# Within each slot of the attention, the value products and exponentials are placed ahead of the output projection

## The reference, cut to what matters

```
x = x + attention(layernorm(x))                # x: 8 sequences of 512 tokens, width 256
    q, k, v = x @ W.T + b                      # 16 query heads, 4 key/value heads, 16 wide
    q, k = rope(q), rope(k)
    att = softmax(causal(q @ k.T / 4))
    y = att @ v
    return y @ Wo.T + bo
x = x + ffn(layernorm(x))
    top 8 of 64 experts per token, softmax of their logits as weights
    out = sum of weight * down(silu(gate(x)) * up(x)) + a shared expert
```

## Time and profile before

| | us |
|---|---|
| median of 3 runs | 1220.87 (1215.87 to 1222.19) |
| the profiled execution | 1212.77 |
| its span, first to last instruction | 1211.0 |
| PE busy | 1023.7 (85%) |
| DVE busy | 710.7 (59%) |
| ACT busy | 676.3 (56%) |
| POOL busy | 723.8 (60%) |

### The profile page before, as it was taken

The page is one execution under the profiler, slowest core; times in us unless marked ns, Lnnn a source line. Parts: engine busy times, 40 slices in busy tenths (PEclk is TensorE's granted clock), DMA queues, the critical chain, the costliest instruction groups (busy, mean ns, idle before and its releaser), DMA issues. The chain is left out here.

```text
span 1211.0 us, 24260 instructions
## 1 busy us (share of the span) xinstructions
PE 1023.7 (85%) x7378; PEld 809.7 (67%) x7378; DVE 710.7 (59%) x2229; ACT 676.3 (56%) x1650; POOL 723.8 (60%) x954
## 2 busy tenths in 40 slices
PE   2799989899989898898998611999999999999962
PEld 1466666666666666666665401999989889999950
DVE  2466776767767677777674550222236656666666
ACT  2366665666656656666554101777656667766630
POOL 3111122774856847658367775577777777777770
PEclk9689999999999999999898855999999999999985
DMA  2388876821312313212132994777778989998735
GB/s 89 131 261 278 270 250 209 285 100 44 112 56 80 118 32 110 83 58 97 39 133 81 323 321 155 217 220 219 219 265 313 374 307 339 316 357 282 260 111 187
DMA packets 142157, 233.23 MB, mean 193 GB/s; under 512 B 17271, under 2 KB 119878, under 8 KB 136656
## 3 DMA queue, kind: packets, MB, share of 16 engines
q1 hardware_dynamic: 67216, 101.06, 25.8%
q0 software_dynamic: 27648, 69.28, 15.8%
q10 hardware_dynamic: 47168, 61.35, 15.3%
HBM read 107.32 MB, written 132.66 MB: 198 GB/s over the span
## 5 line engine op out<-in xcount | busy, mean ns | idle before, releaser
L1363 POOL DMA_INDIRECT res_d<-y,dst_i x320 | 321.6, 1005 | 111.0 <-issue 82.8
L453 POOL DMA_INDIRECT rows_d<-pay,slot_i x256 | 258.4, 1009 | 73.4 <-issue 67.8
L858 DVE TENSOR_REDUCE nmax<-ps 128x1 f32<-128x512 f32 (+3 forms) x448 | 225.6, 530 | 103.7 <-PE ps L508 101.8
L724 ACT ACTIVATE wgu_s<-ps 128x512 f32<-128x512 f32 x320 | 191.3, 599 | 108.2 <-PE ps L508 105.0
L508 PE MATMUL ps<-mask,ident_b 128*128 128x256 bf16 (+1 forms) x640 | 172.2, 269 | 0.0
L501 PE MATMUL ps<-kT,qT 96*128 96x512 f32 (+3 forms) x512 | 166.8, 388 | 6.2 <-DVE nmax L858 4.0
L1294 PE MATMUL psB<-wgu_s,xT 128*128 x1280 | 171.9, 278 | 0.0
L1311 PE MATMUL psD<-wdp_s,innerT 128*128 x640 | 165.7, 382 | 3.7 <-ACT innerT L1199 2.5
L548 PE MATMUL ps<-qT,kT 128*128 128x512 f32 (+3 forms) x512 | 161.3, 377 | 0.9 <-ACT qT L737 0.6
L1294 PEld LDWEIGHTS psB<-wgu_s,xT 128*128 128x128 f32 x1280 | 158.2, 195 | 0.4 <-issue 0.4
L1118 DVE TENSOR_TENSOR inner<-inner,psB 128x128 f32<-128x128 f32 x160 | 45.7, 286 | 188.9 <-ACT inner L1193 185.6
(11 more groups left out here) (241 smaller groups left out, 1622.3 us busy)
## 6 DMA issues: line engine op xcount, KB each, us to landing
rows_d<-blank ACTq DMA_DIRECT2D x8, 5440.0 KB, 19.4
xg<-rows_d SPq DMA_DIRECT2D x160, 272.0 KB
yk<-res_d SPq DMA_DIRECT2D x32, 1024.0 KB
wgu_s<-wgu_in ACTq DMA_DIRECT2D x8, 1024.0 KB, 13.5
xs<-x_d SPq DMA_DIRECT2D x32, 192.5 KB
x_d<-x SPq DMA_DIRECT2D x30, 192.5 KB, 2.5
res_d<-y,dst_i POOLq DMA_INDIRECT x320
wgu_s<-x_in SPq DMA_DIRECT2D x32, 128.0 KB, 2.1
```

The costliest lines, as they stand in the source:

```text
L453: pool.indirect_dma_start(rows_d, bass.IndirectOffsetOnAxis(ap=slot_i[par][:, t, k:k + 1], axis=0), pay[par][:, t, :], None).then_inc(s_sc ...
L724: act.activation(pexp[p % 4][:, s, :], ps2[:, (5 * p + s) % 2, :], ACT.Exp, scale=HEAD_D ** -0.5).then_inc(s_exp, 1)
L858: return dve.tensor_reduce(nmax[u][:, tile, heads[0]:heads[-1] + 1], src, AX.X, ALU.max, negate=True)
L1363: pool.indirect_dma_start(res_d, bass.IndirectOffsetOnAxis(ap=dst_i[:, j % (2 * G):j % (2 * G) + 1], axis=0), y[:, j % Y, :], None, bounds ...
```

## The change

Within `beat`, the call of "products" is moved from the end of the slot to just behind "main", ahead of the calls of "post". Nothing is added or removed. POOL's, SP's and DVE's lists stay as they were, since they have nothing under "products".

```diff
                     steps["main"]((h, par, p) if main else None, *ago, s)
+                    steps["products"](*ago, s)
                     for t in reversed(range(TILES)):
                         k = slot - POST_AT - (POST_EVERY * t if pre else (0, 1, 8, 9)[t] if main else t)
                         if behind and -1 <= k < POST_PARTS:
                             steps["post"](*prv, t, k)
-                    steps["products"](*ago, s)
```

## The result

| | before | after |
|---|---|---|
| median, both kernels timed side by side, 4 runs each | 1218.66 (1215.87 to 1222.19) | 1236.8 (1234.17 to 1244.29) |
| the profiled execution | 1212.77 | 1234.4 |
| its span | 1211.0 | 1232.6 |

The kernel is slower: the ratio is 1.0173 [1.0128, 1.0219], some 18 us where 8 were predicted. The direction is that of the forecast, the size is not.

A forecast was written before the change was run, and what follows sets the result against it. The prediction took PE's list to set the pace. Its terms, 0.35 + 2.0 + 0.25 + 2.2 + 0 + 0.7 + 1.1 + 1.7, made 8.3 us, put on the median of 1220.87: 1229, range 1216 to 1237.

The forecast's parts named there:

- slots 18 and 19: L614 moves behind pass2 and value products; DVE's 1.10 us of idle time before L818 hides it: 0.
- Rival A: Pass2 truly fills post's waits at slots 16 and 26: -4.4 us, clock -3.4, giving 1213; chance 0.17.
- B: Small slack in DVE and POOL absorbs everything, or gains and losses cancel: 0 to +3 us, 1221; chance 0.25.
- slots 13 to 16: At slot 16's wait for pay gain and loss cancel; +0.05 a beat for the matmul turn, seven beats +0.35 us.
- Slots 32 to 36: L614 of slot 32 comes later, DVE stands before L883, ks is late: +0.37 a beat, six beats +2.2 us.
- sign that the wait at slot 36 must rise above 1.95: PE's wait for ks at slot 36 near 2.3 us instead of 1.91; the prediction is wrong if not above 1.95.
- ACT's other copies: Turned copies L772, L775 and L778 wait for PE's post step anyway, with the exponential running beside it: no cost.
- Slot 11: Slots 10 to 12: ACT's oT copy, turned behind the exponential, comes late for L614: +0.1 a beat, +0.7 us.
- Slots 20 to 27: Chain from slot 20's output projection over DVE and POOL to ks at slot 27: +0.4 in beats 2 to 6, +2.0.
- Beat 7: Value products ahead of post at slot 19 delay projections of slots 21 and 22, then col at slot 31: +1.1 us.
- The clock: Longer waits at slot 36 make the clock fall in beats 4 and 5 too: 2 times 0.85, +1.7 us.
- Rival C: The clock also falls at slot 27 in beats 2 to 6: 5 times 0.85 us on top, 1234; chance 0.13.

The follow-up runs named there:

- e7: The changed kernel, but slots 20 and 32 keep the old order on PE and ACT: 1223.87 us, ratio 1.0064 to the kernel before.
- e12: The changed kernel plus the unused matmuls of e10 in PE's waits: 1226.97 us, ratio 1.0078 to the kernel before.
- e10: The kernel before plus unused matmuls on PE at slots 7 (1), 16 (5), 27 (3) and 36 (6): 1209.39 us, ratio 0.9927.
- e9: The changed kernel, but POOL's L431 adds the bias to 16 columns of tile 3 instead of 256: 1232.77 us, ratio 1.0125 to the kernel before.
- e8: The changed kernel with only PE's list in the new order, ACT's in the old: 1233.6 us, ratio 1.0133 to the kernel before.
- e13: The kernel before with the new order at slot 20 alone, plus the unused matmuls of e10: 1209.82 us, ratio 0.9954 to the kernel before.
- e5: The changed kernel plus unused matmuls in PE's waits for ks, 3 at slot 27 and 6 at slot 36: 1232.56 us, ratio 1.0129 to the kernel before.
- e11: The kernel before with the new order at slot 20 alone, on PE and ACT: 1234.07 us, ratio 1.0125.
- e2: The changed kernel with only ACT's list in the new order, PE's in the old, on the slow chip: 1392.86 us, ratio 1.0105 to the kernel before.
- e14: e10 with 3 more unused matmuls at slot 2 and 2 more at slot 7: 1205.48 us, ratio 0.9897 to the kernel before.
- e3: The changed kernel, but slot 20 keeps its old order, on the slow chip: 1388.15 us, ratio 1.0068 to the kernel before.

## Why the prediction was wrong in size

**What held.** The chains were the right ones. DVE stands 0.41 us before L883 of slot 32 (0.37 was said); the waits of slots 26 and 27 grow as a sum; at slot 16 gain and loss cancel (1.32 against 0.44 + 0.90); slots 18 and 19 cost nothing (−0.02 by slot); the experts' stage is unchanged. Keeping slots 20 and 32 as they were gives 11 of 19 us back (e7). Rival A is out: where post's waits were filled, another wait grew. So is B.

**What failed.** Two terms were too small: the waits, the most at slots 32 to 36, and the clock. What the new order costs without the clock can be read slot by slot, e12 less e10 in beats 2 and 4, in which both are at a clock of 1.00 (us a beat):

| slots | forecast | measured |
|---|---|---|
| 0 to 12 | 0.1 | 0.13 |
| 13 to 16 | 0.05 | 0.12 |
| 17 to 19 | 0 | 0.08 |
| 20 to 27 | 0.4 | 0.60 |
| 28 to 31 | 0 | 0.24 |
| 32 to 39 | 0.37 | 1.0 |
| sum | 0.9 | 2.2 |

Up to slot 31 the changed kernel has the same prices wherever its clock is not low. The forecast's 0.05 at slots 13 to 16 stood for a turn between kinds of matmul; no run shows that by itself, the 0.12 holds all causes.

**Slots 32 to 36, 0.37 a beat forecast.** This term was mis-sized. The move by itself costs what was said: in e9 slot 32 is 0.09 longer and slot 34 0.30. But the step took it that DVE's rows behind L883 move back as they are. They don't: L431 on POOL meets L921 and L835, which take up to 1.0 us more (0.82 in beat 3), and slot 34 costs 0.78 to 1.28 in beats 2 to 6. Some 0.4 of that comes back at slots 35 and 38. It also came out at another place, as a wait for `nmax` ahead of slot 35, while that for `ks` fell from 1.91 to 1.77, and is 1.76 in e9 as well. My sign that the wait at slot 36 must rise above 1.95 was wrong for that reason.

**ACT's other copies, forecast as free.** They are not. L775 now stands behind an exponential that pass2 has just released, and PE's L638 waits for it at slot 31, 0.21 by slot; L772 costs 0.17 at slot 13 (e8). I counted the wait for PE's post step, and not that the exponential ahead of the copy is late as well. Slot 24 has the same wait, but there the chain of slot 20 takes it up: without it slot 25 is longer by as much. Slot 11 was right (0.12; 0.1 was said).

**Slots 20 to 27, 0.4 a beat.** Somewhat low: 0.5 to 0.6 by e13.

**Beat 7, +1.1.** The term was right: slots 19 to 38 of the beat are 1.0 us longer, with the wait for `col` at 3.35 instead of 3.01. The beat as a whole is only 0.1 longer, by luck: its slots 0 to 18 are 0.9 shorter, as the clock was low at slot 7 for 3.4 us there instead of 6.8.

**The clock, +1.7.** This is the largest miss. The waits' own price is about 2.2 in each of beats 2 to 6 and 1.2 to 1.3 in beat 1 (75.2 in e12 beside 74.0 in e13 and 73.9 in e10), some 12 us, and 1.0 in beat 7; the forecast had 6.6 for all. Of the 23.3 us of beats 1 to 6 in the profiled execution the other 11 are clock, from 13.6 us at 1.2 GHz to 44. Rival C named the new stretch at slot 27, and it came, but C's price of 0.85 was too low: slot 27 lasts 4.2 us where it is low and 2.66 in beat 4, where it is not, of which slot 28 gives 0.2 back: 1.3. And C stopped there. The fall also came at slot 8 of beat 4, for 1.5 us, and lasted twice as long at slot 35 of that beat. I took the waits as independent spots, each with its own stretch; e5 and e11 speak against it, as the clock fell there at others of the same few waits. The Trainium skill (TensorE: Matmul & The Clock Gate, "A second HAM failure mode: psum-queue depth-cycling") describes throughput lost to going down and up between bursts of matmuls at frequent small idle times. Beat 3 at slot 27 agrees, after waits of 0.69 and 1.19 us; in the prediction I held that the pair didn't, as at 0.81 and 0.82 it had not fallen.

The terms as measured, some 13 of waits and 5 to 10 of clock, make 18 to 23, against 18 by medians and 21.6 in the one profiled execution. The split is by the traces; no pair of runs gives the clock's part of the full change by itself.

**What stays open.** The ACT half alone (e2) was run only on the slow chip. The parts of L431 and of ACT's copies are shown by slots, not in the total. L921 is long even in beat 4, where L431's row begins 0.50 us behind its start; POOL's times are rough, and how the two block each other is left open. In which beats the clock falls differs from run to run by no rule that I found.

## What to carry to other kernels

Where others wait for a step, and the chain behind it has no slack, even 0.4 us of independent work put ahead of it is a loss. Before moving it, follow the chain to the end, through the engines that do not move with it: what will now run beside what, and which copy comes behind which late instruction. And where TensorE's waits recur at fixed places, price the clock over all of them together, compare an edit of the order with the clock held up as well, and try filling the waits with matmuls before reordering.

## What the runs showed of the hardware

- Matmuls whose result nobody uses, put in PE's regular waits, made the kernel 1.0% faster: 0.9897 [0.9853, 0.9941] (e14). The granted clock of beats 1 to 6 was then 1.00 in its trace.
- A low stretch of 3.4 us cost 1.3 to 1.5 us where PE had no further slack (slot 27, 4.2 instead of 2.66 with 0.2 given back behind it; slot 8 of beat 4, 1.5).
- DVE's TENSOR_TENSOR on 128x320 float32 took 1.01 us instead of 0.48, and one on 128x64 0.51 instead of 0.22, beside POOL's TENSOR_TENSOR on 128x256, and their usual times when POOL's had 16 columns (e9); TENSOR_REDUCE from PSUM was not slowed by it (1.34 for three in both).
- One chip ran the same kernel at 1379.53 instead of 1218 us. In a variant's trace from it (e3) most of that lies in the experts' stage, 571 beside 458 us; PE is busy 44 of these 113 us more, at a granted clock of 0.92 beside 0.95, and idle for the rest; the cause is open.
